# Six up-projection blocks moved into the attention, and the reordering around them

## The chip, the cores and the metric

The kernel runs on one NeuronCore of one Trainium2 chip. The metric is the device time of one execution in microseconds (us). Three runs of the kernel before gave 1068.75, 1070.24 and 1074.82 us; the median, 1070.24 us, is the time to compare with.

## The reference

Input: 4 sequences of 1024 tokens, 128 features, float32. Four residual sublayers follow one another, each `x = x + layernorm(f(layernorm(x)))`:

1. a single-head attention over channels;
2. a feed-forward layer with ternary weights and an exact gelu;
3. an attention with 16 heads of 8 features and rotary positions;
4. a mixture of 24 experts, cut to what matters here:

```python
def per_group(xf, lw, lb):                       # 4 groups of 1024 tokens
    combine, dispatch = top2_dispatch(xf, Wg, C) # softmax gates, top 2, capacity C = 86 per expert
    h = moe_apply(xf, combine, dispatch, W1, b1) # per expert 128 -> 512, summed over a token's 2 experts
    h = layer_norm(h, lw, lb)
    h = jax.nn.relu(h)
    return moe_apply(h, combine, dispatch, W2, b2)  # 512 -> 128
```

A token's hidden row is the sum of two experts' outputs, and the normalisation comes after that sum. A group is the same quarter of all four sequences.

## The kernel before, in words

The change lies in the last two stages, `second_scores` (L1581, the 16-head attention) and `expert_layers` (L1940, the experts). Each is a block with one hand-written instruction list per engine; an engine goes on to the next block when all have finished. Nothing is scheduled by a tool: the order is what the code says, and engines wait on semaphores.

**The attention** works in 8 halves (`HB`), half k being one sequence's 512 query tokens. A half has 32 steps (`G`), 8 for each of 4 units of 4 heads. I number steps through: step 32k + g. In each step TensorE computes four 128x512 score tiles (`score`, L1846, two per call), ScalarE exponentiates them in two 128x1024 instructions (L1676), and TensorE multiplies the exponentials of two steps back with the values (`av`, L1859, 8 matmul records). PSUM has 8 banks: three score buffers of two banks (`RING`), and two banks `acc` in which units accumulate in turn. VectorE copies a finished unit out of its `acc` bank, TensorE transposes it into a ring slot (L1866), VectorE divides (L1770, L1773). Four products per half, in `LATE` steps 6, 8, 22 and 25 (`late_products`, L1492 to L1496: two groups of transposes, the output projection, the gate logits), belong to the half before; the VectorE class `LateChain` continues them with two normalisations and the top-2 search (`choices`). TensorE, VectorE and SyncE issue these in order, so an instruction that waits holds all behind it.

**Routing.** `Choice` turns the expert choices of two groups into lists of rows: `prefixes`, `positions`, `gates`, `values`, `spread` on VectorE, and `position_products`, `map_products` (L1468), `last_products` (L1479) on TensorE. Its last step sets `rows_done`. Groups 0 and 1 are routed in halves 4 to 7 (`routes`, L1870), in the unused bank of an output slot; groups 2 and 3 in the expert stage, once half 7's late products and their VectorE chain are through. After routing, GpSimd gathers the input rows of the first four blocks (L1726), and SyncE loads the remaining W2 experts at the end of the attention (L1666).

**The experts** work in 24 blocks (`NU`), 6 per group (`NB`), each 4 experts of 96 rows in three 128-row tiles. For block n: GpSimd gathers its input rows (`gather_x`); TensorE transposes them (L2153) and computes the up layer (`up`, L2156: per tile 8 float32 matmul records and 4 bfloat16 bias products); ScalarE scales them by the gate into a ring of 27 row tiles in SBUF (`hidden`, L2259); SyncE stores each tile to `h_rows` in HBM. When the whole group is stored, GpSimd gathers for each row the other expert's row of that token (`partners`, L2076): in `ACCUMULATED` blocks, 0 to 5 among them, an indirect DMA adds it in place; otherwise it goes to a buffer and VectorE adds. ScalarE squares and sums (`std`, L2278), VectorE scales (`normed`), TensorE transposes (`h_transposes`), ScalarE applies scale, bias and relu (`relu`, L2291), TensorE computes the down layer (`down`, L2192, L2196), VectorE scales (`result`) and SyncE stores.

GpSimd's order is a fixed list (from L2105): x-gathers 4 to 9, partners 0 to 3, x 10, partners 4, x 11, partners 5, x 12 to 15, partners 6 and 7, and so on. TensorE's order (from L2209) interleaves up(0) to up(5) with the four late products of half 7, then up(6), positions of groups 2 and 3, up(7), up(8), routes(2), down(0), up(9), routes(3), down(1), up(10), down(2), up(11), down(3) to down(5). From down(6) on, groups overlap: three ups ahead, then one beside each of three downs.

## Time and profile before

| | us |
|---|---|
| Median of 3 runs | 1070.24 |
| Profiled execution, span on the chip | 1135.4 |
| Sublayers 1 and 2 and the projections of 3 | 0 to 239.5 |
| Attention: first exponential to the end of the last unit | 239.5 to 731.7 |
| Experts | 731.7 to 1135.4 |
| TensorE busy | 908.8 (80%) |
| ScalarE busy | 774.8 (68%) |
| VectorE busy | 580.1 (51%) |
| POOL (GpSimd) busy | 353.7 (31%) |

The profiled execution's own time is its span; it is 65.2 us longer than the median of the unprofiled runs. How to read the profile: each instruction has a start and a duration; the idle time before it is put down to the instruction or transfer whose semaphore came last; "issue" means that nothing in the profile was waited for, and "remote" that what ended the wait isn't told. PE is TensorE's matmuls and PEld its weight loads, ACT is ScalarE, DVE VectorE, POOL GpSimd. PEclk 1.00 is the full granted TensorE clock. TensorE's ends are modelled, so the distance between starts is the safer measure.

### The profile page before, as it was taken

Reading aid. Unit: us, or ns where it says so; the run is one execution under the profiler, and the core shown is the slowest. Engines: PE = TensorE matmul, PEld = TensorE weight load, DVE = VectorE, ACT = ScalarE, POOL = GpSimd, SP = SyncE. Lnnn points to the kernel's source line nnn. Section 1 sums busy time; section 2 is a strip of 40 time slices with the busy share of each in tenths; the row PEclk is TensorE's granted clock in tenths of the full one; section 3 lists DMA queues with packets and bytes.
Section 4 is the critical chain, followed back from the end, with each engine's and each line's share of the span. In section 5 each row is a group of like instructions: output and inputs, shape, how many; then the busy total and the mean of one; then the engine's idle time right before and its main releaser. Section 6 shows DMA issues by size and latency. Waiting matters only on the chain. (4 is left out here: it accounts for less than half of the span.)

```text
span 1135.4 us, 19356 instructions
## 1 busy us (share of the span) xinstructions
PE 908.8 (80%) x6642; PEld 428.2 (38%) x6642; DVE 580.1 (51%) x1969; ACT 774.8 (68%) x1130; POOL 353.7 (31%) x335
## 2 busy tenths in 40 slices
PE   3959878859999999998999999887876488477830
PEld 3745664312222222222222233224563265357730
DVE  7499998931144444444342624255214036476667
ACT  1236555789999999999999999746444254455510
POOL 6322445831000000000000013147746735365733
PEclk9669988969999999999999999998889688898975
DMA  5000001544541211212121213668747436375741
GB/s 166 1 1 1 1 1 50 130 111 153 154 118 43 61 42 40 56 36 54 44 62 44 58 36 83 184 188 198 143 127 229 88 114 178 95 192 156 144 118 51
DMA packets 91325, 106.56 MB, mean 94 GB/s; under 512 B 12957, under 2 KB 63902, under 8 KB 91114
## 3 DMA queue, kind: packets, MB, share of 16 engines
q1 hardware_dynamic: 77512, 76.83, 22.9%
q0 software_dynamic: 12224, 27.80, 12.0%
q10 hardware_dynamic: 1506, 0.89, 0.3%
q8 instruction: 44, 0.72, 0.3%
q14 instruction: 39, 0.32, 0.1%
HBM read 68.90 MB, written 36.57 MB: 93 GB/s over the span
## 5 line engine op out<-in xcount | busy, mean ns | idle before, releaser
L1676 ACT ACTIVATE s_e<-s_ps 128x1024 f32<-128x1024 f32 x512 | 476.7, 1065 | 12.3 <-PE s_ps L1846 11.5
L1859 PE MATMUL s_acc<-s_e,s_v 128*32 128x512 f32 x2048 | 274.0, 607 | 0.7 <-ACT s_e L1676 0.7
L1293 POOL DMA_INDIRECT x_in<-x_tokens,rows_of x72 | 72.2, 1003 | 458.7 <-DVE rows_of L1449 416.3
L1846 PE MATMUL s_ps<-qk 51*128 51x512 bf16 x1024 | 180.2, 387 | 23.1 <-ACT s_e L1676 10.4
L1846 PEld LDWEIGHTS s_ps<-qk 51*128 51x128 bf16 x1024 | 41.2, 93 | 272.8 <-ACT s_e L1676 252.2
L2291 ACT ACTIVATE qk<-e_pn,ln_hid 128x384 f32<-128x384 f32 x96 | 63.4, 667 | 89.7 <-remote 38.9
L2196 PE MATMUL e_py<-w,qk 128*96 128x128 f32 x768 | 112.3, 298 | 0.5 <-issue 0.5
L2166 PE MATMUL e_ph<-w,qk 128*32 128x512 f32 x576 | 84.9, 654 | 31.9 <-ACT e_hs L2259 23.9
L2196 PEld LDWEIGHTS e_py<-w,qk 128*96 128x96 f32 x768 | 101.6, 184 | 0.8 <-issue 0.8
L1293 POOL DMA_INDIRECT e_ya<-y_rows,take x64 | 63.0, 985 | 40.5 <-issue 19.4
L2259 ACT ACTIVATE e_hs<-e_ph,gate_of 128x512 f32<-128x512 f32 x54 | 36.3, 687 | 56.8 <-PE e_ph L2169 31.3
L1859 PEld LDWEIGHTS s_acc<-s_e,s_v 128*32 128x32 f32 x2048 | 40.4, 108 | 80.3 <-issue 53.5
L2180 PE MATMUL e_pn<-ident,e_hs 128*128 128x128 f32 x216 | 41.3, 313 | 35.8 <-ACT qk L2291 19.9
L1770 DVE RECIPROCAL s_rec<-s_ps 128x16 f32<-128x16 f32 x32 | 8.2, 258 | 107.6 <-PE s_ps L1866 107.5
L1293 POOL DMA_INDIRECT v_all<-h_rows,rows_of x39 | 39.1, 1002 | 75.5 <-DVE x_res L2340 21.3
L1293 POOL DMA_INDIRECT e_hs<-h_rows,rows_of x30 | 50.5, 1684 | 19.7 <-DMA h_rows<-e_hs 8.0
L1758 DVE COPY s_as<-s_acc 128x512 f32<-128x512 f32 x32 | 22.1, 689 | 65.1 <-PE s_acc L1859 64.4
L2180 PEld LDWEIGHTS e_pn<-ident,e_hs 128*128 128x128 f32 x216 | 29.3, 160 | 39.8 <-ACT qk L2291 22.0
L2269 ACT ACTIVATE l_o<-e_hs 128x512 f32<-128x512 f32 x54 | 33.7, 625 | 10.2 <-DMA e_hs<-h_rows,rows_of 5.8
L2166 PEld LDWEIGHTS e_ph<-w,qk 128*32 128x32 f32 x576 | 15.7, 114 | 64.4 <-ACT e_hs L2259 35.4
L1513 DVE COPY s_ot<-s_ps 128x512 f32<-128x512 f32 x14 | 9.7, 692 | 45.8 <-PE s_ps L1492 45.8
L2169 PE MATMUL e_ph<-bias_split,expert_hot 128*32 128x512 bf16 x288 | 31.8, 406 | 0.6 <-issue 0.6
(459 smaller groups left out, 1422.7 us busy)
## 6 DMA issues: line engine op xcount, KB each, us to landing
h_rows<-e_hs SPq DMA_DIRECT2D x54, 256.0 KB
w<-in_w SPq DMA_DIRECT2D x10, 768.0 KB, 6.1
qk<-parts_k SPq DMA_DIRECT2D x64, 96.0 KB
qk<-parts_k SPq DMA_DIRECT2D x64, 64.0 KB
h_rows<-x_res SPq DMA_DIRECT2D x16, 256.0 KB
parts_q<-b_parts SPq DMA_DIRECT2D x16, 192.0 KB, 2.8
parts_k<-b_parts SPq DMA_DIRECT2D x16, 192.0 KB, 2.8
qk<-parts_q SPq DMA_DIRECT2D x64, 48.0 KB
```

The costliest lines, as they stand in the source:

```text
L1293: nc.gpsimd.indirect_dma_start(dst, None, rows, bass.IndirectOffsetOnAxis(ap=idx, axis=0), compute_op=op).then_inc(R["landed"][k % FLIGHT] ...
L1676: nc.scalar.activation(E[g % 4][:, 2 * pair:2 * pair + 2, :], pS[BUFFER["score", 2 * g + pair]][:].rearrange("p (a s) -> p a s", a=2), ACT ...
L1758: nc.vector.tensor_copy(AS[hu % 2][:], acc[hu % 2][:]).then_inc(acc_read, 1)
L1846: last = nc.tensor.matmul(pS[BUFFER["score", 2 * g + pair]][:, a * CH:(a + 1) * CH], K[c % 2][rows, pair, j * P:(j + 1) * P], Q[c % 2][row ...
L1859: last = nc.tensor.matmul(acc[hu % 2][32 * h:32 * h + 32, :], V4[c % 2][:, j, h, :], E[g % 4][:, h, :], start=j == 0, stop=j == TB - 1)
L2166: mm(pH[m % 2][32 * q:32 * q + 32, :], XT[n % 2][:, j * P + 32 * q:j * P + 32 * q + 32], W1[:, e, :], start=True, stop=False)
L2169: last = mm(pH[m % 2][32 * q:32 * q + 32, :], I3[:, e:e + 1].broadcast_to([P, 32]), BS[:, 0:FF], start=False, stop=True)
L2180: tr = nc.tensor.transpose(pN[k % 2][:, j * P:(j + 1) * P], row(m * TPB + j)[:, c * P:(c + 1) * P], ident[:])
L2196: last = mm(out[0:ROWS, e * D:(e + 1) * D], HT[c][:, e * ROWS:(e + 1) * ROWS], W2[:, eb * EB + e, c, :], start=False, stop=c == FC - 1, sk ...
L2259: nc.scalar.activation(row(m), pH[m % 2][:], ACT.Copy, scale=G128[:, n // NB, m % NT:m % NT + 1]).then_inc(hs_done, 1)
L2269: nc.scalar.activation(squares, row(t), ACT.Square, accum_out=ssq[:, t % NT:t % NT + 1]).then_inc(sq_done, 1)
L2291: nc.scalar.activation(HT[c][:].rearrange("p (g j s) -> p j g s", g=EB, j=TPB), src, ACT.Relu, bias=lnh[:, 1, h, c:c + 1], scale=lnh[:, 0, ...
```

## The change

- The attention is unrolled from half 4 on (before: 5). In the unrolled halves the product with the values that would stand in step 8c + 2 comes one step later, so that a unit can begin in the bank that the unit before has just left; from half 4's third unit all units use `acc[0]`, and `acc[1]` is a spare bank.
- Routing of groups 0 and 1 goes through the spare bank at steps 160 to 184, in half 5; the mean-centring of W1 is spread over halves 1 to 3 (before: 1 to 4).
- From step 191 on, in three of eight steps, TensorE issues one of 24 pieces in the spare bank: for each of blocks 0 to 5 the input transposes and three up tiles. VectorE reads each piece (`up_read`): a copy, or the gate scaling into one of four staging tiles. GpSimd stores the tile to `h_rows`, and gathers x 4 to 9 there too. W2's rest is loaded at step 192.
- In the expert stage SyncE first loads the 18 tiles of blocks 0 to 5 back (`own_load`). TensorE does the late products, waits until they are read, then down(0), positions, up(6), routes(2), up(7), down(1), up(8), routes(3), up(9), down(2), up(10), down(3), up(11), down(4), down(5). The positions of groups 2 and 3 share one bank, one after the other. From block 6's down on, the order is the old one. ScalarE starts with std(0), std(1), relu(0), and VectorE interleaves `normed` and `result` with the routing.

```diff
+UB = 6
+UNROLLED = 4
+SINGLE = UNROLLED * HU + 2
+ROUTE_STEPS = {"places": (160, 162), "rows": ((170, 172), (181, 183)), "tiles": (173, 184)}
+UP_STEPS = [s for s in range(191, G * HB) if s % TB in (2, 5, 7)][:UB * (TPB + 1)]
+NST = 4
...
+        single = lambda k, hu: isinstance(k, int) and k * HU + hu >= SINGLE
+        acc_of = lambda k, hu: acc[0] if single(k, hu) else acc[hu % 2]
+        spare = acc[1]
+        XT = R["V"][:, 0:NQ].rearrange("p n t e -> p (n t e)")[:, 0:TPB * P]
+        staged = [R["X"][:, b * TB:b * TB + TH, :].rearrange("p t d -> p (t d)") for b in range(NST)]
...
+                if n == 6 * NQ + 1:
+                    sp.wait_ge(split_done, 6)
+                    sp.wait_ge(R["rows_done"], 2)
+                    w2(slice(EARLY, NE))
...
-                landed(pool, R, place("x", 0, TPB * n + TPB - 1))
+            for n in range(UB):
+                for t in range(n * TPB, (n + 1) * TPB):
+                    pool.wait_ge(u_read, t + n + 2)
+                    nc.gpsimd.dma_start(DR["h"][t // NT][t % NT, :, :], staged[t % NST]).then_inc(R["st_out"][t % NST], 16)
+                if n + NXS < 2 * NB:
+                    if n + NXS == NB:
+                        pool.wait_ge(R["rows_done"], 2)
+                    pool.wait_ge(u_mm, n * (TPB + 1) + 1)
+                    gather_x(nc, R, n + NXS)
...
+            def up_read(step):
+                if step not in UP_STEPS:
+                    return
+                i = UP_STEPS.index(step)
+                n, j = i // (TPB + 1), i % (TPB + 1) - 1
+                v.wait_ge(u_mm, i + 1)
+                if j < 0:
+                    nc.vector.tensor_copy(XT, spare[:, 0:TPB * P]).then_inc(u_read, 1)
+                    return
+                t = n * TPB + j
+                if t == 0:
+                    v.wait_ge(R["x_saved"], 16 * B)
+                if t % NT == 0:
+                    v.wait_ge(R["rows_done"], t // NT + 1)
+                if t >= NST:
+                    v.wait_ge(R["st_out"][t % NST], 16 * (t // NST))
+                nc.vector.tensor_scalar(staged[t % NST], spare[:], R["G128"][:, t // NT, t % NT:t % NT + 1], None,
+                                        ALU.mult).then_inc(u_read, 1)
...
+            def first_unit(k, at):
+                unit_read(k, 0)
+                up_read(at + 10)
+                chain.output_statistics(k - 1)
+                chain.inverse_deviation()
+                unit_output(k, 0)
+                up_read(at + 12)
+                if k == 5:
+                    choice.map_rows(0, spare)
+                chain.output_normed()
+                if k == 5:
+                    choice.last_rows(0, spare)
+                up_read(at + 13)
+                chain.residual(k - 1)
+                up_read(at + 15)
+                chain.inverse_deviation()
+                chain.normed(k - 1)
+                up_read(at + 16)
...
+                if k == 4:
+                    choice.prefixes()
+                    choice.positions(0, spare)
...
+            def fourth_unit(k, at):
+                unit_read(k, 3)
+                up_read(at + 10)
+                if k == 4:
+                    choice.positions(1, spare)
+                    choice.gates()
+                unit_output(k, 3)
+                up_read(at + 12)
+                if k == 4:
+                    choice.values()
+                up_read(at + 13)
+                if k < HB - 1:
+                    chain.read(k, 0)
+                if k == 4:
+                    choice.spread(0)
+                up_read(at + 15)
+                if k < HB - 1:
+                    chain.read(k, 1)
+                up_read(at + 16)
...
+            def route(step):
+                if step in ROUTE_STEPS["places"]:
+                    h = ROUTE_STEPS["places"].index(step)
                     pe.wait_ge(R["pf_done"], 1)
+                    if h == 0:
+                        pe.wait_ge(acc_read, SINGLE)
+                    else:
+                        pe.wait_ge(R["pos_read"], h)
...
+                        position_products(nc, R, W, spare, h, i)
+                for h in range(2):
+                    if step == ROUTE_STEPS["rows"][h][0]:
+                        pe.wait_ge(R["hot_done"], 2 * (h + 1))
+                        if h == 0:
+                            pe.wait_ge(R["pos_read"], 2)
+                        else:
+                            pe.wait_ge(R["rows_done"], h)
+                        map_products(nc, R, W, spare, h, range(GT))
+                    if step == ROUTE_STEPS["rows"][h][1]:
+                        map_products(nc, R, W, spare, h, range(GT, 2 * GT))
+                    if step == ROUTE_STEPS["tiles"][h]:
+                        last_products(nc, pe, R, W, spare, h)
...
+            def early_up(step):
+                if step not in UP_STEPS:
+                    return
+                i = UP_STEPS.index(step)
+                n, j = i // (TPB + 1), i % (TPB + 1) - 1
+                if i == 0:
                     pe.wait_ge(R["rows_done"], 2)
+                    pe.wait_ge(w1_done, NE // 3)
+                    pe.wait_ge(split_done, 6)
+                    pe.wait_ge(one_done, 4)
+                else:
+                    pe.wait_ge(u_read, i)
+                if j < 0:
+                    for t in range(TPB):
+                        landed(pe, R, place("x", n // NB, n % NB * TPB + t))
+                    for t in range(TPB):
+                        tr = nc.tensor.transpose(spare[:, t * P:(t + 1) * P], R["XS"][n % NXS][:, t, :], R["ident"][:])
+                    tr.then_inc(u_mm, 1)
+                    return
+                up_products(nc, R, spare, XT, n, j).then_inc(u_mm, 1)
...
+                    if unrolled and g % TB == 3:
+                        av(k, first, g - 3)
+                    if not unrolled and (g >= 2 or not first) or unrolled and g % TB != 2:
...
+                    if unrolled:
+                        route(k * G + g)
+                        early_up(k * G + g)
...
-            return range(m + NB, m + NR) if m % NB == 0 and m + NB < NU else ()
+            return range(m + NB, m + NR) if m in (NB, 2 * NB) else ()
 
         def beside(m):
 
+            if m < NB:
+                return {0: (6, 7), 1: (8, 9), 2: (10,), 3: (11,)}.get(m, ())
...
+            for i in range(NST):
+                sp.wait_ge(R["st_out"][i], staged_count(i, UB * TPB))
             for n in range(NB):
-                h_store(n)
-                if n == 3:
-                    token_rows(sp, R, HB - 1)
+                own_load(n)
+            token_rows(sp, R, HB - 1)
+            sp.wait_ge(R["x_out"], 16 * HB)
+            sp.wait_ge(R["x_saved"], 16 * HB)
...
+                for i in range(NST):
+                    if h < 2:
+                        pool.wait_ge(R["st_out"][i], staged_count(i, min(UB, (h + 1) * NB) * TPB))
+                if (h + 1) * NB > UB:
+                    pool.wait_ge(h_out[h], 16 * TPB * ((h + 1) * NB - max(UB, h * NB)))
                 for t in range(first * TPB, end * TPB):
                     n = kept_adds(t)
                     if t // TPB in ACCUMULATED:
                         dst, op = row(t), ALU.add
+                        if t // TPB < UB:
+                            pool.wait_ge(own_in[t // TPB], 16 * TPB)
...
-            inputs(4, 10)
...
+            def positions():
+                pe.wait_ge(R["pf_done"], 2)
+                for h in (2, 3):
+                    if h == 3:
+                        pe.wait_ge(R["pos_read"], h)
+                    for i in range(GT):
+                        position_products(nc, R, W, pM, h, i)
...
-            late(0)
-            x_transposes(0)
-            for n in range(NB):
-                up(n)
-                if n in (0, 3, 4):
-                    late({0: 1, 3: 2, 4: 3}[n])
+            for i in range(NX):
+                late(i)
+            pe.wait_ge(R["late_read"], HB * NX)
+            for c in range(FC):
+                h_transposes(0, c)
+            pe.wait_ge(R["w2_in"], 48)
             for m in range(NU):
-                for n in ahead_of(m)[0:1]:
+                for n in ahead_of(m):
                     up(n)
-                if m == 0:
-                    pe.wait_ge(R["pf_done"], 2)
-                    for h in (2, 3):
-                        for i in range(GT):
-                            position_products(nc, R, W, pY[h - 2], h, i)
-                for n in ahead_of(m)[1:]:
-                    up(n)
-                if m == 0:
-                    routes(2)
-                if m % NB == 0:
+                if m and m % NB == 0:
                     for c in range(FC):
                         h_transposes(m, c)
-                if m == 0:
-                    pe.wait_ge(R["w2_in"], 48)
                 for c in range(FC):
                     down(m, c)
-                    if m % NB < NB - 1:
+                    if m == 0 and c == FC - 1:
+                        positions()
+                        h_transposes(1, FC - 2)
+                    if m % NB < NB - 1 and (m or c != FC - 2):
                         h_transposes(m + 1, c)
-                for n in beside(m):
+                if m == 0:
+                    x_transposes(NB)
+                for i, n in enumerate(beside(m)):
                     up(n)
-                if m == 0:
-                    routes(3)
+                    if m < 2 and i == 0:
+                        routes(m + 2)
...
-            xt(0)
-            for n in range(NB):
-                hidden(n)
+            act.wait_ge(R["late_mm"], HB * NX - 3)
+            std(0)
+            std(1)
+            relu(0, NU)
             exponents(nc, act, R, 1)
-            act.wait_ge(R["late_mm"], HB * NX - 1)
-            act.wait_ge(R["x_out"], 16 * HB)
-            for h in range(GR):
+            std(2)
+            for j in range(NB):
+                if j < NB - 1:
+                    relu(j + 1, j + 3)
+                if j == 0:
+                    xt(NB)
+                for n in beside(j):
+                    hidden(n)
...
+            normed(0)
             chain.read(p, 3)
+            normed(1)
             chain.choices(p)
             choice.prefixes()
-            choice.positions(2, pY[0])
-            choice.positions(3, pY[1])
+            choice.positions(2, pM)
+            choice.positions(3, pM)
             choice.gates()
+            normed(2)
+            result(0)
             choice.values()
             choice.spread(2)
+            normed(3)
             choice.map_rows(2, pM)
             choice.last_rows(2, pM)
-            normed(0)
             choice.spread(3)
-            normed(1)
-            normed(2)
-            result(0)
+            result(1)
+            normed(4)
             choice.map_rows(3, pM)
             choice.last_rows(3, pM)
-            normed(3)
-            result(1)
-            normed(4)
+            result(2)
             normed(5)
-            for j in range(2, NB - 1):
-                result(j)
+            result(3)
```

## Rows read from the trace of the kernel before

**Rows 1.** Windows cut at the starts of halves 1, 4, 5, 6, 7: us, busy (records), PEclk, DMA, GB/s

```profile
299.50:359.40 59.90, 57.51 (x426) 14.66 (x424) 26.42 (x94) 59.41 (x65) 0.00 (x0) 1.00 0.37 103
479.40:542.60 63.20, 58.04 (x432) 14.84 (x434) 29.08 (x105) 60.27 (x67) 0.00 (x0) 1.00 0.18 47
542.60:603.00 60.40, 58.23 (x470) 15.87 (x468) 21.74 (x98) 59.49 (x65) 0.00 (x0) 1.00 0.18 50
603.00:665.40 62.40, 60.41 (x458) 17.43 (x456) 28.95 (x114) 59.64 (x65) 0.00 (x0) 1.00 0.17 48
665.40:728.30 62.90, 60.55 (x505) 17.82 (x504) 20.30 (x95) 59.88 (x65) 12.06 (x12) 1.00 0.48 125
```

**Rows 2.** Timeline, attention half 6, ScalarE and TensorE: start us, us, engine, line, operation

```profile
601.22 18.63 ACT L1676 ACTIVATE s_e<-s_ps 128x1024 f32<-128x1024 f32 x20
...
615.57 1.06 PE L1859 MATMUL s_acc<-s_e,s_v 128*32 128x512 f32 x8
...
617.10 1.06 PE L1859 MATMUL s_acc<-s_e,s_v 128*32 128x512 f32 x8
...
618.42 0.97 PEld L1494 LDWEIGHTS s_ps<-l_wo,s_ot 128*128 128x128 f32 x8 [0.23 <-issue]
```

**Rows 3.** Timeline, half 4, VectorE

```profile
535.05 1.90 DVE L1375 TENSOR_TENSOR w<-w 128x96 bf16<-128x96 bf16 x8
```

**Rows 4.** Timeline, half 6, TensorE

```profile
656.33 2.86 PE L1468 MATMUL s_ps<-w 128*96 128x72 f32 x32
```

**Rows 5.** Timeline, end of the attention, TensorE's weight loads

```profile
731.73 0.42 PEld L1492 LDWEIGHTS e_pn<-ident,l_o 128*128 128x128 f32 x4 [1.16 <-issue]
```

**Rows 6.** Timeline of the expert stage, TensorE

```profile
818.58 0.49 PE L2153 MATMUL e_px<-ident,x_in 128*128 128x128 f32 x3
819.00 1.06 PE L2166 MATMUL e_ph<-w,qk 128*32 128x512 f32 x8
...
820.10 1.04 PE L2166 MATMUL e_ph<-w,qk 128*32 128x512 f32 x8
...
822.37 0.42 PE L2192 MATMUL e_py<-bias_split,expert_hot 128*96 128x128 bf16 x4
...
827.46 0.49 PE L2153 MATMUL e_px<-ident,x_in 128*128 128x128 f32 x3
...
836.84 1.93 PE L2166 MATMUL e_ph<-w,qk 128*32 128x512 f32 x8 [6.25 <-ACT e_hs L2259]
...
851.73 3.69 PE L2196 MATMUL e_py<-w,qk 128*96 128x128 f32 x32
```

**Rows 7.** Waits of ScalarE after 731 us: us in total, times, longest us

```profile
ACT qk L2291 <- remote: 38.9, 10, 8.2
...
ACT e_hs L2259 <- remote: 24.3, 7, 7.8
```

**Rows 8.** Timeline, POOL (the waits before each in brackets)

```profile
693.86 1.42 POOL L1293 DMA_INDIRECT x_in<-x_tokens,rows_of  x1 [2.55 <-DMA x_in<-x_tokens,rows_of]
...
770.29 1.60 POOL L1293 DMA_INDIRECT e_hs<-h_rows,rows_of  x1 [7.96 <-DMA h_rows<-e_hs]
...
799.40 0.95 POOL L1293 DMA_INDIRECT x_in<-x_tokens,rows_of  x1 [0.30 <-issue]
...
842.26 0.95 POOL L1293 DMA_INDIRECT v_all<-h_rows,rows_of  x1 [7.73 <-DMA h_rows<-e_hs]
```

**Rows 9.** Timeline of the expert stage, ScalarE and TensorE's weight loads

```profile
789.38 0.30 ACT L2275 ACTIVATE gate_exponents<-gate_exponents,consts 128x3 f32<-128x3 f32 x1
...
791.95 1.72 PEld L2196 LDWEIGHTS e_py<-w,qk 128*96 128x96 f32 x8
```

**Rows 10.** Timeline of the expert stage, VectorE

```profile
763.64 0.44 DVE L1560 MAX8 l_top<-l_lg 128x8 f32<-128x24 f32 x4
...
771.76 1.02 DVE L1384 TENSOR_TENSOR v_all<-e_py,e_ya 128x384 f32<-128x384 f32 x2 [3.15 <-PE e_py L1459]
...
779.22 1.35 DVE L1430 TENSOR_TENSOR v_all<-e_ya 128x1152 f32<-128x1152 bf16 x1
```

211 lines of the change are left out of this document (99 added, 112 removed).

## The prediction

> **What bounds the kernel now.** I read the busy table in windows first, cut where the halves of the attention begin. A plain half takes 59.9 us, ScalarE busy 59.4 of it, at the full TensorE clock [rows 1]. Then the timeline of one half: 20 exponentials in 18.63 us with the last one's own 1.0, so one per about 0.92 us and 1.84 us per step [rows 2]. So ScalarE bounds the attention. TensorE is close behind: two products with the values start 1.53 us apart where nothing holds it [rows 2]. Three unrolled halves are longer than 59.9: half 4 with 63.2, half 6 with 62.4, half 7 with 62 [rows 1]. In half 4 VectorE makes the prefixes of the routing, 1.90 us for their additions alone, ahead of a unit's output [rows 3]; in halves 6 and 7 TensorE has a 2.86 us row of map products [rows 4] between scores.
>
> In the expert stage, from 731.7 us on [rows 5], nothing is busy throughout. Partners of group 0 can be gathered only when all its up tiles are stored, at 770.3; those of group 1 start at 842.3 [rows 8]. TensorE begins down(0) at 792 [rows 9] and ends down(5) at 851.73 + 3.69 = 855.4 [rows 6]. ScalarE's waits there have an odd part: 38.9 and 24.3 us on which the profile names no cause [rows 7]. The same table for the attention has none of these, and their sum, 63 us, is nearly the 65.2 us by which the profiled span exceeds the median. I take these stalls for a cost of being profiled. That matters here: a trade in the expert stage has to be made in time without them.
>
> **Step 1: what the attention pays.** A half costs TensorE 32 x 1.53 = 49.0 us, four output transposes and two transposing late products of 0.42 each (the same operation as in [rows 5]) = 2.5, and the two other late products near 1.0 each [rows 2] = 2.0: 53.5 us. An up tile costs 820.10 - 819.00 = 1.10 us, an input transpose 0.42 [rows 6].
> - Halves 6 and 7 get 18 up tiles and 5 transposes: 19.8 + 2.1 = 21.9. Together 2 x 53.5 + 21.9 = 128.9 us against 62.4 + 62.9 less 1.1 (the window of half 7 runs to the last product), 124.2 now: +4.7. TensorE is then the bound in both.
> - Half 5 gets the map products, 2 x 2.86 [rows 4], about 0.8 for the small tile products, 1.4 for the positions (my estimate, half of the late ones), one transpose: 53.5 + 8.3 = 61.8 against 60.4: +1.4.
> - Half 4 loses its stall, since the prefixes now follow the output: -3.
> - The product that waits a step puts two (2 x 1.0 us) between the two scores of step 8c + 3. The ring holds ScalarE's work for at most two exponentials, 1.84 us. Halves 4 and 5, where TensorE has room otherwise, may lose 0 to 1 us in each of 8 units; I take 0.4, +3.
>
> Sum: **+6**. Bounds: 0 if the doubled products and half the pieces fit where TensorE waits now; +15 if VectorE's read of the spare bank holds TensorE by a further 0.4 us in each of 24 pieces. VectorE reads 18 x 0.7 + 6 x 0.5 = 16 us more, in program order with a chain of some 4 us between two unit reads; it is under half busy (29 of 62 us [rows 1]), and pieces stand over 3.7 us apart, so I expect little of it. SyncE's W2 load moves from behind the last q/k loads to before them; DMA is 0.17 busy in half 6 [rows 1], and a load has a whole unit, 15 us, so I cost it at nothing. Without that room the next unit's scores would wait for it.
>
> **Step 2: the store path.** GpSimd is idle in halves 4 to 6 [rows 1]; it gets 18 stores and 18 more gathers there. A gather occupies it up to 1.42 us in the attention [rows 8]. A block, 3 stores and 3 gathers, must take less than four pieces, 10.7 steps or 21 us; at 1.42 + 0.3 each it is 10. It costs nothing. The Trainium skill speaks against it (SBUF — State Buffer, the trap "DVE blocks DMA"): a DMA issued by GpSimd that takes 620 ns alone took about 3100 ns beside VectorE copies. By that page, an estimate, a block would take 6 x 3.1 = 18.6 us and still fit, barely. No row here shows such a wait, so the rival that uses it gets little.
>
> **Step 3: the expert stage before, without the stalls.** From 731.7: one up block with its transpose takes 822.37 - 818.58 = 3.8 us, a down block with the next transposes 827.46 - 822.37 = 5.1 [rows 6]. Six ups and the late products, 22.8 + 3.3, and about 5 for the last scaling and store put the partners' start at 763 (trace: 770.3). From that start to the square root of block 1 took 789.4 - 770.3 = 19.1 us, and 2.6 more to down(0) [rows 8, 9]: 784.7. down(0) 5.1; then up(9) waits for gather x 10, which stands behind 12 partner gathers: the trace has its last issue 29.1 us after the first partner [rows 8], so 792, landed at 796.5; up(9) 3.8, routes(3) 3.4, four more downs 20.4 and two ups 7.6, less what already overlaps, plus some 4 for x 11: down(5) ends at about 836, the partners of group 1 start at about 825. The trace has 855.4 and 842.3: 19 and 17 us of stalls in the first 124 of 404 us, in proportion to 63.
>
> **Step 4: the same with the change.** The stage begins at 731.7 + 6 = 737.7. What is late next is the round trip: group 0's tiles are in HBM and must come back. Three 256 KB loads with their latency, about 5 us (estimate), then the same 19.1 + 2.6: down(0) at 764.4, 20 us earlier. But only six ups are done, where before nine were. The routing now sets the pace: VectorE needs normed(1) (1.5), then from choices to spread(2) what the trace takes, 779.22 + 1.35 - 763.64 = 16.9, less its 3.15 wait [rows 10], plus about 3 for positions one after the other in one bank and 2.2 for normed(2) and result(0): 782.5. TensorE has down(0), positions and up(6) in that time, 11 us of 18, and waits. Then routes(2) 3.5, five ups 19.0, five downs 25.5, routes(3) 3.4: 834; down(5) ends there, and the partners of group 1 start after up(11), at about 827.
> The idle 20 us at the start also cools TensorE: after 6.25 us of idle an up tile took 1.93 instead of 1.06 us [rows 6], and the granted clock is at its lower level, 1.2 GHz, for the first few microseconds. +2 us. So 836 against 836, 829 against 825.
>
> Nothing behind it changes in kind: block 6 needs TensorE free, which weighs as much as the partners. I take the end of down(5): **0 us**. Against the median: **1070**. A measurement of this kernel tells about 0.5% (5.3 us) from no change.
>
> **The rivals.**
> - *The stalls are the kernel's own* (or shrink with the stores that leave). Then before is 855.4 as traced, and after has its 97 us of path from 737.7, plus 10 rather than 19 of stalls: 845, so -10, 1060. For it: the stalls stand beside heavy DMA traffic, and 4.6 MB of stores leave the stage. Against: equally many bytes are loaded back, and the sum of 63 fits the profiling. Some gain would also come from the attention's lower bound (0, not +6). Together **0.36**, from 1052 to 1064.9.
> - *TensorE-bound attention with held reads*, the one on the other side. Place: halves 6 and 7, where TensorE no longer has room. If a piece waits for VectorE's read, 24 x 0.4 = 9 more; the attention is then 15 longer, 1079; to 1086 if the round trip also meets its own loads, 18 of them in a row, and takes 7 more. It decides from 0.25 us per piece. For it: VectorE's order is fixed, and `up_read` waits for a piece while the chain behind it waits. Against: pieces are spaced. **0.25.**
> - *The GpSimd path fills* (the page's rule): a block over 21 us would stop staging, reads, and TensorE; at 4 us each six operations take 24, 3 us per block, 15 in all: 1085. **0.02.**
> - *It doesn't do what it says*: the ups could stand in the attention and still end later than it. Program order excludes that: the expert block starts only when TensorE has issued all 24 pieces, so it would show as a longer attention, and is in the second rival.
>
> My forecast, an even trade within 0.5%, has **0.37**. Its own range is 1065 to 1076. The whole range holds the first rival's 1056 and most of the second's: **1056 to 1083**. Outside it lie about 0.08 below and 0.08 above. Faster by over 0.5%: 0.36; within: 0.37; slower: 0.27 (0.25 + 0.02).
>
> **What the profile of the changed kernel would show.**
> - Half 4 near 60 us, halves 6 and 7 near 65 each, with ScalarE waiting for scores and TensorE's starts without gaps. Halves of 60 would mean step 1 is too dear; waits of TensorE for `up_read` would make the second rival.
> - No TensorE work between the late products and down(0) but transposes, about 20 us, and a PEclk under 1.0 there. First partner gather about 5 us after the stage begins, down(0) 26 to 27 us after it.
> - TensorE waiting for spread(2) ahead of routes(2), rows_done for group 2 about 50 us into the stage.
> - down(5) ending about 97 us after the stage's start, plus stalls. If this is under 90, step 4 is wrong; if the whole stage after it is shorter or longer than before's 280 us (1135.4 - 855.4), I have missed what follows.

## The result, and the profile after

The changed kernel takes 1086.84 us, the median of four runs (1081.79 to 1090.62), against 1072.2 of four of the kernel before: 1.0147 of it, 95% interval 1.0114 to 1.0179. I had forecast 1070.0 with 1056 to 1083. In a later comparison on the same kind of chip it was 1.0156 (1.0126 to 1.0187). The profiled execution took 1081.79 us with a span of 1079.9, so its parts add up without the 65 us that stood between trace and median before. It is the fastest of the four, though, 5 us under their median.

First the windows of the plain half 1 and of halves 4 to 7 of after, cut at the same exponentials as [rows 1]:

```profile
core 0: us, PE busy (x) PEld busy (x) DVE busy (x) ACT busy (x) POOL busy (x), PEclk, DMA share, GB/s
296.50:356.40 59.90, 57.58 (x426) 14.70 (x424) 26.42 (x94) 59.41 (x65) 0.00 (x0) 1.00 0.34 103
476.40:537.10 60.70, 57.19 (x446) 15.43 (x445) 22.42 (x101) 60.16 (x66) 0.00 (x0) 1.00 0.18 50
537.10:602.80 65.70, 63.78 (x572) 22.57 (x568) 32.95 (x129) 60.52 (x66) 12.50 (x12) 1.00 0.23 57
602.80:672.50 69.70, 68.58 (x545) 18.56 (x541) 27.81 (x102) 61.58 (x66) 12.91 (x17) 1.00 0.51 151
672.50:742.20 69.70, 68.50 (x544) 18.07 (x536) 27.05 (x100) 61.58 (x65) 13.85 (x18) 1.00 0.27 76
```

Half 4 fell from 63.2 to 60.7 us, half 5 grew from 60.5 to 65.7, halves 6 and 7 from 62.4 and 62.8 to 69.7 each. In these two TensorE is busy for all but 1.1 us, at the full clock, while ScalarE, which bounds half 1, is idle for 8 us. VectorE is busy for 28 of 69.7 us. What TensorE waits for in half 6, and how long (summed us, times, longest), is one row, and none of it is a wait for VectorE's reads:

```profile
PE s_ps L1955 <- ACT s_e L1701: 1.0, 3, 0.5
```

The timeline of TensorE's matmuls in half 6 shows what one piece costs (start, duration, line, operation, count):

```profile
603.01 0.60 PE L1955 MATMUL s_ps<-qk 51*128 51x512 bf16 x4
603.55 1.06 PE L1968 MATMUL s_acc<-s_e,s_v 128*32 128x512 f32 x8
...
611.32 0.66 PE L1975 MATMUL s_ps<-ident,s_as 128*128 128x128 f32 x4
611.91 0.39 PE L1955 MATMUL s_ps<-qk 51*128 51x512 bf16 x2
612.23 1.06 PE L1968 MATMUL s_acc<-s_e,s_v 128*32 128x512 f32 x8
613.22 0.39 PE L1955 MATMUL s_ps<-qk 51*128 51x512 bf16 x2
613.54 1.07 PE L1317 MATMUL s_acc<-w,v_all 128*32 128x512 f32 x8
614.43 0.40 PE L1320 MATMUL s_acc<-bias_split,expert_hot 128*32 128x512 bf16 x4
614.76 0.39 PE L1955 MATMUL s_ps<-qk 51*128 51x512 bf16 x2
615.08 1.06 PE L1968 MATMUL s_acc<-s_e,s_v 128*32 128x512 f32 x8
```

Read distances between starts. Four scores side by side take 603.55 - 603.01 = 0.54 us. An up tile (L1317 and L1320) takes 614.76 - 613.54 = 1.22, and it stands between two pairs of scores: they take 2 x 0.32 (613.22 to 613.54, 614.76 to 615.08) instead of 0.54. Together 1.32 us. The output transposes take 0.59 and split the scores in the same way.

Then the expert stage, TensorE's matmuls at its start and at down(5):

```profile
744.20 0.66 PE L1975 MATMUL s_ps<-ident,s_as 128*128 128x128 f32 x4 [0.81 <-DVE s_as L1786]
747.48 0.82 PE L1512 MATMUL e_pn<-ident,l_o 128*128 128x128 f32 x4 [2.63 <-PEq L1603]
749.09 2.08 PE L1514 MATMUL e_pn<-l_wo,v_all 128*128 128x128 f32 x8 [0.78 <-DVE v_all L1533]
763.53 1.12 PE L1512 MATMUL e_pn<-ident,l_so 128*128 128x128 f32 x4 [12.36 <-DVE l_so L1572]
...
794.01 4.05 PE L1488 MATMUL e_pm<-v_all 128*96 128x72 f32 x32 [3.05 <-DVE v_all L1450]
...
843.74 3.69 PE L2328 MATMUL e_py<-w,qk 128*96 128x128 f32 x32
```

and GpSimd's first partner gather:

```profile
754.40 1.62 POOL L1301 DMA_INDIRECT e_hs<-h_rows,rows_of  x1 [6.14 <-DMA e_hs<-h_rows]
```

The stage's start (L1512, the row that answers to [rows 5]) is at 747.48, the first partner 6.9 us behind it, the end of down(5) at 847.43, 99.95 us behind. For 12.36 us TensorE waits for VectorE's chain. In the 28.1 us from the stage's start to down(0) it is busy for 8.8, so idle for 19.3, at a granted clock of 0.51; I had forecast about 20 us idle and a clock under 1.0.

These lengths need a trace of before without the stalls of [rows 7]. It came with the experiments: prefixes_2 below is the kernel before with one VectorE step moved, and differs from it in half 4 alone (60.6 instead of 63.2). Its rows of TensorE:

```profile
726.28 0.63 PE L1492 MATMUL e_pn<-ident,l_o 128*128 128x128 f32 x4 [0.94 <-PEq L1583]
...
828.72 3.69 PE L2196 MATMUL e_py<-w,qk 128*96 128x128 f32 x32
```

| us | before | after | difference | forecast |
|---|---|---|---|---|
| halves 4 and 5 | 123.7 | 126.4 | +2.8 | +1.4 |
| halves 6 and 7 | 125.2 | 139.5 | +14.3 | +4.7 |
| end of the last exponential to the stage's start | 3.5 | 5.2 | +1.7 | 0 |
| stage's start to end of down(5) | 106.1 | 99.95 | -6.2 | -6 |
| from there to the end | 230.6 | 232.5 | +1.9 | 0 |

(The first three lines of before are from its own trace, the last two from prefixes_2: 832.41 - 726.28, 1063.0 - 832.41.) The sum is +14.5 us, and 1.47% of 1070 is 15.7. The last line is the least certain. The trace of after_2 below, a run at its kernel's median, has the same attention and the same 99.9 us to down(5), but 236.5 us from there to the end instead of 232.5, and the other kernels with six blocks in the attention have 235.8 to 237.8 on that kind of chip (piece_beside, ups_first, both_edits). Kernels with the old stage have 230.6 (prefixes_2) and 232.9 (reorder_spread). So behind down(5) the changed kernel more likely loses some 4 us than 2. Why, no run here tells. The switch of blocks is longer because TensorE idles 2.63 us for its own queue there (the row at 747.48) and 0.94 in the other kernel.

### The profile page after: what moved, and what is told of

Read it like the earlier page. It is cut to its first block and busy times, and to the rows that moved or that the text cites. A ratio compares the mean times of both kernels' runs of the same rounds, so it can differ in the third digit from the quotient of the medians.

```text
span 1079.9 us, 19334 instructions
## 1 busy us (share of the span) xinstructions
PE 888.2 (82%) x6642; PEld 418.2 (39%) x6642; DVE 598.5 (55%) x1993; ACT 766.9 (71%) x1108; POOL 365.5 (34%) x353
## 5 line engine op out<-in xcount | busy, mean ns | idle before, releaser
L1968 PE MATMUL s_acc<-s_e,s_v 128*32 128x512 f32 x2048 | 270.6, 606 | 0.5 <-ACT s_e L1701 0.4
L2328 PE MATMUL e_py<-w,qk 128*96 128x128 f32 x768 | 104.0, 284 | 0.0
L2328 PEld LDWEIGHTS e_py<-w,qk 128*96 128x96 f32 x768 | 93.8, 172 | 0.0
L1301 POOL DMA_INDIRECT e_ya<-y_rows,take x64 | 65.6, 1025 | 32.5 <-issue 25.3
L1317 PE MATMUL e_ph<-w,qk 128*32 128x512 f32 x432 | 62.6, 654 | 7.3 <-ACT e_hs L2396 5.5
L1756 POOL DMA_DIRECT2D h_rows<-x_res x18 | 10.2, 564 | 127.6 <-DVE x_res L1816 127.6
L2396 ACT ACTIVATE e_hs<-e_ph,gate_of 128x512 f32<-128x512 f32 x36 | 24.4, 688 | 16.9 <-PE e_ph L1320 15.9
L2483 DVE TENSOR_TENSOR e_hs<-e_hs,v_all 128x512 f32<-128x512 f32 x24 | 16.2, 691 | 26.9 <-DMA v_all<-h_rows,rows_of 26.8
L759 PEld LDWEIGHTS a_po<-down_t,f_h 128*128 128x128 f32 x256 | 29.7, 192 | 2.9 <-issue 2.9
```

What stands on the lines that cost most here:

```text
L759: last = mm(pD[k % 2][:, j * P:(j + 1) * P], H[:, k % 2, f, j * P:(j + 1) * P], R["down_t"][:, f * P:(f + 1) * P], start=f == 0, stop=f == ...
L1301: nc.gpsimd.indirect_dma_start(dst, None, rows, bass.IndirectOffsetOnAxis(ap=idx, axis=0), compute_op=op).then_inc(R["landed"][k % FLIGHT] ...
L1317: nc.tensor.matmul(bank[32 * q:32 * q + 32, :], XT[:, j * P + 32 * q:j * P + 32 * q + 32], R["W1"][:, e, :], start=True, stop=False)
L1968: last = nc.tensor.matmul(acc_of(k, hu)[32 * h:32 * h + 32, :], V4[c % 2][:, j, h, :], E[g % 4][:, h, :], start=j == 0, stop=j == TB - 1)
L2328: last = mm(out[0:ROWS, e * D:(e + 1) * D], HT[c][:, e * ROWS:(e + 1) * ROWS], W2[:, eb * EB + e, c, :], start=False, stop=c == FC - 1, sk ...
L2396: nc.scalar.activation(row(m), pH[m % 2][:], ACT.Copy, scale=G128[:, n // NB, m % NT:m % NT + 1]).then_inc(hs_done, 1)
```

## The experiments

The theory (A): the loss is made in the attention by TensorE's own time, since halves 6 and 7 became TensorE-bound and each piece costs more than its duration; the expert stage gives what I forecast up to down(5). Rivals: the reordering itself costs (C), the pieces wait for VectorE's read (D), the stalls of ScalarE (E). Further letters are explained in the expectation in which they stand.

**Two kinds of chip.** The comparisons ran on chips of two kinds. On one the kernel before took 1128.33 us (median of 23 runs, 1121 to 1140), on the other 1070.08 (19 runs, 1065 to 1075). I tell the kinds apart by this time alone; all comparisons of the slower kind are of one chip. The ratios below are to the kernel before on the same chip.

**The kernel before again.** No edit.

> The kernel before, unchanged, for a trace that can be compared with that of after. Theory A (the 15 us are lost in the attention, which grew from 487.7 to 504.7 us between first and last exponential; the expert stage is an even trade): the attention takes 487 to 489 us again, without a stall without a named cause in the expert stage, and the expert stage, from the last unit's transposes to the end, takes about 332 us, as it does after. Rival B (the expert stage lost too, or gained and gave part back): that stage takes under 328 or over 337 us here.

Measured: 1127.57 us. The waits of ScalarE in its trace, the answer to [rows 7] (summed us, times, longest):

```profile
ACT qk L2291 <- remote: 42.4, 12, 10.3
...
ACT e_hs L2259 <- remote: 25.5, 9, 6.4
```

The stalls are back, and on this chip all other runs take about 1128 us too. None of the eight traces of the faster kind, which are profiled as well, has a row with "remote". So the stalls are a matter of the chip or its state, not of profiling; the trace of before that I had read shows the same stalls and length. The attention took 488.6 us between first and last exponential, as expected; the stage can't be compared on this chip.

**The reordering alone, without pieces.** The attention of after without a piece, the expert stage of before, and GpSimd waits after each of its first gathered blocks, as in before.

```diff
-UP_STEPS = [s for s in range(191, G * HB) if s % TB in (2, 5, 7)][:UB * (TPB + 1)]
+UP_STEPS = []
...
             for n in range(NXS):
                 gather_x(nc, R, n)
+                landed(pool, R, place("x", 0, TPB * n + TPB - 1))
```

> The reordered attention of after (unrolled from half 4, one accumulator bank and a spare one, the two products of the values in steps 8c + 3, routing of groups 0 and 1 through the spare bank in half 5, prefixes behind the output), with no up tile in it; the expert stage is that of before. Theory A (the inserted pieces make the loss): half 4 stays near 60.7, half 5 near 65, halves 6 and 7 fall from 69.7 to 60 us each; the whole 3 us under before, ratio 0.997. Rival C (the doubled products and the single accumulator make it): halves 6 and 7 stay above 63 us, the whole at 1075 or more.

Measured (slower chip): 0.9949 (0.9912 to 0.9986). Halves 6 and 7:

```profile
606.80:667.00 60.20, 56.69 (x426) 14.94 (x424) 19.74 (x90) 59.69 (x66) 0.00 (x0) 1.00 0.47 128
667.00:727.00 60.00, 56.05 (x422) 14.73 (x420) 19.54 (x89) 59.49 (x65) 0.00 (x0) 1.00 0.14 39
```

The doubled products, the single accumulator and the W2 load at step 192 cost nothing there; C is out. Half 5 took 68.8 us, 3 more than in after; on the faster chip it was never over 65.7 in any kernel.

**The map products spread over two halves.** The same, with the steps of group 1's map products moved by 32 and the W2 load at the end again.

```diff
-ROUTE_STEPS = {"places": (160, 162), "rows": ((170, 172), (181, 183)), "tiles": (173, 184)}
+ROUTE_STEPS = {"places": (160, 162), "rows": ((170, 172), (213, 215)), "tiles": (173, 216)}
```

> The reordered attention without the pieces, as before, with the map products of group 1 in half 6 instead of half 5, and the load of the rest of W2 at the end of the attention again. Theory A: half 5 falls from 65 (68.8 as run) to about 62.5, half 6 grows from 60.1 to about 62.5, since what counts is the ring running dry at each row of 1.4 us; the whole equals reordering alone or is 1 to 3 us shorter, 0.993 to 0.997 of before. Rival C (half 5 is long because TensorE has too much to do there in all): the two halves together lose 4 us or more.

Measured (faster chip): 0.9979 (0.9959 to 0.9999), halves 5 to 7 of 62.4, 63.4 and 60.3 us. The two halves lose 2.4 + 3.4 = 5.8 us over 60, as much as half 5 of after alone. That passes the 4 us which I had put down as the sign of rival C (too much TensorE work in half 5), but my own theory gave some 5, so the sign couldn't tell them apart. What speaks against C is that half the work in each of two halves costs as much as all of it in one. My 62.5 for half 6 was low, and nothing is gained: behind each map row of 1.43 us ScalarE waits 0.9 to 1.2 us, about 1.1, wherever it stands. That is what is left of 1.43 if the ring refills by only 1.84 - 1.53 = 0.3 us per step (an estimate). In before an undivided row of 2.86 us costs 2.4 a half. Splitting rows saved nothing, and the 5.7 us of half 5 are for the most part the price that halves 6 and 7 had paid before.

**Up tiles without their float32 products.**

```diff
-    for q, e in enumerate(experts):
+    for q, e in enumerate(experts if full else ()):
         nc.tensor.matmul(bank[32 * q:32 * q + 32, :], XT[:, j * P + 32 * q:...], R["W1"][:, e, :],
```

> After, but the 18 up tiles in the attention consist of their bfloat16 bias products alone: the eight float32 matmul records of each tile, the product of the tokens with W1, are left out, so the hidden rows of blocks 0 to 5 hold the bias only. Everything that waits, reads, stores and gathers stays. Theory A (TensorE's own time is the price, with what a change of shape costs it): a tile gets cheaper by about 0.85 us and there are 9 in each of halves 6 and 7; these fall from 69.7 to about 62, at most 7.7 less each, and the whole is 15 us under after, near 1071. Rival D (the wait for VectorE's read of the spare bank, or its place in VectorE's order, is the price): the halves stay above 66 us and the whole above 1080.

Measured (slower chip): 0.9979 (0.9937 to 1.0021). Windows of halves 5 to 7, and one tile in TensorE's timeline:

```profile
539.00:618.80 79.80, 66.93 (x571) 22.85 (x567) 33.02 (x129) 61.10 (x66) 11.55 (x12) 0.89 0.20 47
618.80:681.20 62.40, 60.72 (x473) 17.14 (x469) 27.71 (x102) 60.51 (x65) 12.92 (x17) 1.00 0.57 168
681.20:743.80 62.60, 60.76 (x472) 16.74 (x464) 26.94 (x100) 60.65 (x65) 13.86 (x18) 1.00 0.30 85
```

```profile
628.92 0.40 PE L1320 MATMUL s_acc<-bias_split,expert_hot 128*32 128x512 bf16 x4
629.26 0.39 PE L1955 MATMUL s_ps<-qk 51*128 51x512 bf16 x2
```

A tile is 0.34 us instead of 1.22: 9 x 0.88 = 7.9 us less work per half, and the halves fell by 7.1 to 7.3. What TensorE is spared comes off by nine tenths, with every wait, read, store and gather still there. Half 5 (79.8 us here, clock 0.89) is taken up under two_blocks.

**Each tile read twice by VectorE.**

```diff
+                nc.vector.tensor_copy(junk[:], spare[:])
                 nc.vector.tensor_scalar(staged[t % NST], spare[:], R["G128"]...).then_inc(u_read, 1)
```

> After, but VectorE reads each of the 18 up tiles in the spare bank twice, the first time into scratch space, and says only then that the bank is free: some 0.65 us more per tile, 12 us more of VectorE. Theory A: TensorE is the bound and a piece stands over 3.7 us behind the one before, so nothing or up to 2 us is added. Rival D (the pieces wait for VectorE's read): the 0.65 us come back for most of 18 tiles, 8 to 12 us.

Measured (slower chip): 1.0147 (1.0093 to 1.0202). Halves 6 and 7 in windows:

```profile
618.70:688.50 69.80, 68.68 (x545) 18.64 (x541) 33.10 (x111) 61.68 (x66) 12.56 (x17) 1.00 0.51 150
688.50:758.20 69.70, 68.51 (x544) 18.16 (x536) 32.35 (x109) 61.57 (x65) 13.85 (x19) 1.00 0.26 77
```

VectorE does 5.3 us more per half than in after and the halves stay at 69.7. TensorE's waits in half 6 are those of after, 1.0 us in three pieces for ScalarE, and none for the reads. D, the mechanism of my second rival, is out.

**After again**, beside the next ones on the faster chip.

> After, unchanged, beside the kernels of this comparison, on a chip where the kernel before may take longer for the stalls of ScalarE. All theories: halves 6 and 7 at 69.7 us. Theory A: the loss of the attention is there whatever the chip, so the ratio is 1.005 to 1.02. Theory E (the first profile of before was of a chip with these stalls, and what a kernel loses to them depends on where its GpSimd gathers stand): halves 4 and 5 or the expert stage differ from the first trace of after by 5 us and more where ScalarE waits without a named cause.

Measured: 1.0156 (1.0126 to 1.0187), 1087.6 us; all halves as in the first trace within 0.1 us, down(5) ends 99.9 us behind the stage's start. No ScalarE wait without a cause, so E's difference isn't seen between two chips of this kind.

**Pieces next to the products with the values.**

```diff
                         av(k, first, g - 2)
+                    if unrolled:
+                        early_up(k * G + g)
                     score(k, first, g, 1)
...
                         route(k * G + g)
-                        early_up(k * G + g)
```

> After, but each of the 24 pieces is issued right behind the product with the values (in steps 8c + 2, which have none, between the two scores) instead of behind the step's second score, so that the scores of two steps stay next to each other and a float32 128 x 32 product follows one of the same shape. Theory A (a piece costs TensorE 0.2 us more than its own time, for the change of shape and for the scores that no longer overlap): 12 pieces in each of halves 6 and 7 get 0.15 to 0.25 us cheaper, these halves fall from 69.7 to 66.7 to 67.9, the whole by 4 to 6 us. Rival F (the halves are long by the pieces' own time and by waits for ScalarE's tiles): no change, within 0.5 us per half, or slower since the second score comes later in the step.

Measured: 1.0077 (1.0050 to 1.0105), 1080.4 us. Halves 6 and 7 took 67.2 us. The timeline of half 6:

```profile
620.20 1.06 PE L1968 MATMUL s_acc<-s_e,s_v 128*32 128x512 f32 x8
...
621.08 1.04 PE L1317 MATMUL s_acc<-w,v_all 128*32 128x512 f32 x8
...
622.27 0.61 PE L1955 MATMUL s_ps<-qk 51*128 51x512 bf16 x4
622.81 1.07 PE L1968 MATMUL s_acc<-s_e,s_v 128*32 128x512 f32 x8
```

The product with the values is 0.88 us to the next start instead of 0.99 (612.23 to 613.22 above), the tile 1.19, and the scores stay four in 0.54. So a tile costs 1.19 - 0.11 = 1.08 instead of 1.32 us, 9 x 0.24 = 2.2 of the 2.5 us per half. The rest of the 7 us of the whole was unexpected: down(5) ended 96.2 us behind the stage's start instead of 99.9, with no edit there. The map row of routes(2), here and in after_2:

```profile
791.45 2.94 PE L1488 MATMUL e_pm<-v_all 128*96 128x72 f32 x32 [1.00 <-DVE v_all L1450]
795.73 3.94 PE L1488 MATMUL e_pm<-v_all 128*96 128x72 f32 x32 [3.36 <-DVE v_all L1450]
```

It took 2.94 us at a granted clock of 1.00 where it follows 1.00 us of idle; in after_2 it follows 3.36 us and took 3.94, at 0.70, and the 6 us behind it stood at 0.65. From this row to down(1), the same instructions, piece_beside takes 7.7 us and after_2 10.6: these 2.9 us of clock are most of the 3.7, and behind down(1) the two run alike.

**up(6) and up(7) into the wait at the stage's start.**

```diff
-            for i in range(NX):
-                late(i)
+            late(0)
+            late(1)
+            x_transposes(NB)
+            up(NB)
+            up(NB + 1)
+            late(2)
+            late(3)
```

> After, with up(6) and up(7) moved from behind the positions and routes(2) to the start of the expert stage, into the 12.4 us that TensorE waits there for the chain of VectorE; they fit, since the first seven halves of x are saved at the end of the attention. The attention does not change. Theory A (after down(0) TensorE's list of products is the path to down(5): five ups, five downs, two routings behind spread(2)): down(5) ends 4 to 8 us earlier than in after (100 us behind the stage's start), and so does the kernel. Rival G (routing on VectorE and the partner gathers on GpSimd set the pace up to down(5)): under 2 us.

Measured: 1.0091 (1.0060 to 1.0121), 1081.5 us. TensorE's wait of 12.36 us has gone:

```profile
763.80 0.40 PE L1320 MATMUL e_ph<-bias_split,expert_hot 128*32 128x512 bf16 x4
764.37 0.66 PE L1512 MATMUL e_pn<-ident,l_so 128*128 128x128 f32 x4 [0.17 <-DVE l_so L1572]
...
796.10 1.24 PE L1488 MATMUL e_pm<-v_all 128*96 128x72 f32 x6 [5.57 <-DVE v_all L1450]
```

The stage began at 748.76, down(5) ended at 840.24 + 3.69 = 843.93, 95.2 us behind it instead of 99.9: 4.7 us, of 7.6 moved. The third row shows where the rest went: routes(2) now waits 5.57 us for spread(2), with nothing left to do meanwhile. Both the products behind down(0) and the routing of VectorE set the pace, and my G (the routing sets it) is right for what goes beyond 4.7.

**Both edits, first on the slower chip.** The two diffs above together.

> After with both edits: pieces right behind the products with the values, and up(6), up(7) at the start of the expert stage. Theory A (the two act in different stages): halves 6 and 7 at 67.2 us as with the first alone, down(5) ends 95 us or less behind the stage's start as with the second alone; 10 to 13 us under after, 1.003 to 1.007 of before. Rival H (both repair the same thing, the cold clock of TensorE behind the wait of 12 us): 7 to 8 us under after.

Measured: 1.0105 (1.0058 to 1.0152), halves 6 and 7 of 67.2 and 67.5 us. Down(5) ended 108.5 us behind the stage's start there, with stalls of ScalarE inside, in a run 12 us above the median, so this says little on the stage.

> The kernel of beside_and_first again. On a chip without the stalls, theory A: 10 to 13 us under after, 1.002 to 1.006 of before; rival H (both edits repair the cold clock): 1.007 to 1.009. On a chip with them only the halves 6 and 7 and the first 100 us of the stage can be read.

Measured (faster chip): 1.0053 (1.0032 to 1.0073), 1076.7 us. Halves 67.2 each, down(5) 94.9 us behind the start. Against 1.0156 that is 1.03% or 11 us. The halves keep their 5.0. In the stage the two together give 5.0, where the one alone gave 4.7 and the other 3.7: there both repair partly the same thing, as H says, and A holds for the attention. The row of routes(2) shows how: it took 5.39 us behind 5.71 of idle, at a clock of 0.50, as in ups_first, so that nothing is left of piece_beside's warm row. The 11 us of the whole fit A's 10 to 13.

**The prefixes behind the output of unit (4, 2), in the kernel before.**

```diff
-                    if (k, hu) == (4, 2):
-                        choice.prefixes()
                     v.wait_ge(tr_mm, k * HU + (hu + 1))
...
                                         ALU.mult).then_inc(o_done, 1)
+                    if (k, hu) == (4, 2):
+                        choice.prefixes()
```

> The kernel before with one edit: the prefixes of the routing behind the output of unit (4, 2) instead of ahead of it. All theories: half 4 from 63.2 to 60 to 60.7 us, nothing else moves; the whole 2.5 to 3 us under before, 0.997, that is, all of what the reordered attention brings.

> The kernel of prefixes again. Half 4 at 60.6 us and the others as in before, the whole at 0.997 of before on a chip without stalls; theory E: the stalls of ScalarE stay away or come as they do for before.

Measured: 0.9944 (0.9900 to 0.9989) on the slower chip, 0.9972 (0.9954 to 0.9990) on the faster, where it took 1067.36 us. Half 4 fell to 60.6 us, the others stayed: 2.6 us for one moved call, as much as the whole reordered attention brings without pieces.

**Two blocks instead of six.** Eight pieces, in step 8c + 2 of halves 6 and 7, between the two scores. The expert stage computes the other four blocks first, takes up(6) to up(8) ahead of down(0), and puts normed(0) and normed(1) ahead of spread(2).

```diff
-UB = 6
-UP_STEPS = [s for s in range(191, G * HB) if s % TB in (2, 5, 7)][:UB * (TPB + 1)]
+UB = 2
+UP_STEPS = [s for s in range(191, G * HB) if s % TB == 2][:UB * (TPB + 1)]
...
+            late(0)
+            x_transposes(UB)
+            for n in range(UB, NB):
+                up(n)
+                if n == UB:
+                    late(1)
+            late(2)
+            up(NB)
+            late(3)
+            up(NB + 1)
+            positions()
+            up(NB + 2)
...
+                if m == 0:
+                    routes(2)
+                for n in beside(m):
+                    up(n)
+                if m == 0:
+                    routes(3)
```

> Two blocks instead of six in the attention: eight pieces, one per unit, each in step 8c + 2 between the two scores, where no product with the values stands. up(2) to up(5) in the expert stage with the late products between them, up(6) to up(8) behind, then down(0), routes(2), up(9), routes(3), and on as before. Theory A (up to 4 pieces per half fit into the 4 us that TensorE has over; what costs is the pieces above that): halves 6 and 7 at 60 to 61.5 us, the first partner gather 22 to 25 us behind the stage's start instead of 35, down(5) 96 to 100 us behind it instead of 106, the whole at 0.990 to 0.996 of before. Rival G (the routing chain of VectorE sets the pace and the gain is given back behind down(5)): 0.996 to 1.000.

Measured (slower chip): 0.9989 (0.9942 to 1.0036), no change clear of noise. Halves 6 and 7 took 61.3 us, as expected, but half 5 took 79.8. So did it in every kernel on this chip that issues the first 12 gathers in a row (bias_tiles, twice_read, beside_and_first), against 68.8 in reorder_only, which waits for each block, and 65.7 in all of them on the faster chip. In twice_read ScalarE's rows there are:

```profile
576.88 1.94 ACT L1702 ACTIVATE s_e<-s_ps 128x1024 f32<-128x1024 f32 x2 [4.55 <-remote]
585.48 3.77 ACT L1702 ACTIVATE s_e<-s_ps 128x1024 f32<-128x1024 f32 x4 [6.66 <-remote]
```

Both waits begin within the row of gathers (568.2 to 583.1). So I let GpSimd wait for each block again:

```diff
             for n in range(NXS):
                 gather_x(nc, R, n)
+                landed(pool, R, place("x", 0, TPB * n + TPB - 1))
```

> Two blocks in the attention as in two_blocks, and the first 12 gathers of GpSimd in half 5 wait for each block to land again, as in the kernel before (after lets all 12 go in a row). Theory A: halves 6 and 7 at 61.3 us, down(5) 96 to 101 us behind the stage's start on a chip without stalls of ScalarE (106 in the reordered kernel without pieces), the whole at 0.990 to 0.997 of before. Theory E (on a chip with the stalls, the row of 12 gathers brings 14 us of them into half 5): half 5 near 66 to 69 us on either chip, against 79.8 for the row of 12 on the chip with stalls. Rival G (given back behind down(5)): 0.997 to 1.001.

Measured (faster chip): **0.9915** (0.9892 to 0.9939), 1061.57 us, faster than both kernels. The windows of halves 5 to 7:

```profile
538.90:604.60 65.70, 63.78 (x572) 22.40 (x567) 32.40 (x128) 60.53 (x65) 14.17 (x12) 1.00 0.23 57
604.60:665.90 61.30, 60.41 (x465) 15.97 (x463) 22.49 (x94) 59.78 (x65) 4.65 (x6) 1.00 0.52 142
665.90:727.30 61.40, 59.93 (x461) 15.74 (x459) 22.29 (x93) 59.88 (x65) 4.64 (x6) 1.00 0.19 54
```

and TensorE at the stage's start and at down(5):

```profile
730.93 0.63 PE L1512 MATMUL e_pn<-ident,l_o 128*128 128x128 f32 x4 [0.94 <-PEq L1603]
...
772.06 3.18 PE L2322 MATMUL e_pn<-ident,e_hs 128*128 128x128 f32 x12 [6.25 <-DVE e_hs L2506]
...
821.37 3.69 PE L2338 MATMUL e_py<-w,qk 128*96 128x128 f32 x32
```

The middle row is TensorE's longest wait on the way, 6.25 us for the scaling of block 0 ahead of down(0). Four pieces a half cost 1.2 us over the 60.1 without any; twelve in the same place, between the two scores, cost 7.1 (67.2 in piece_beside), and 9.6 where after has them. The partners start 23.5 us behind the stage's start (32.6 in prefixes_2, 6.9 in after), down(5) ends at 94.1 instead of 106.1. The whole, against the same two traces as in the table: attention and switch +0.7 (492.9 against 492.2 from the first exponential to the stage's start), -12.0 up to down(5), +3.3 behind it (233.9 against 230.6): -8.0, and 0.85% is 9.1. Of these, some 3 us are the moved prefixes, which this kernel has too: against prefixes_2, which took 1067.36 us on the same chip, it wins 5.8 us. Whether pacing removes the 14 us on the slower chip wasn't tried: this run was on the faster one.

## Why the prediction was wrong

Step 1 failed: its term for halves 6 and 7, 64.5 us each, measured 69.7, which is 10.4 of the 16.8 us that were missing (1086.8 - 1070). The price of a piece in its place had been taken too low. Half 5 adds 3.9 (65.7 - 61.8), the switch of blocks 1.7. Step by step:

- *Step 1, halves 6 and 7: wrong in size.* The mechanism was right (TensorE the bound, full clock, nearly no gaps), the term was 64.5 us per half and measured 69.7. I took durations from stretches in which TensorE does the same thing over and over, and none for going from one to the other. An up tile was 1.10 and is 1.32 with the scores that it parts (9 x 0.22 = 2.0); output transposes were 0.42 and are 0.59, plus 0.10 for the parted scores (4 x 0.27 = 1.1); the late products and the input transposes lose in the same way (about 1.5 together, my estimate from the same distances). With 1.1 us of waits for ScalarE that is 5.7, against 5.2 missing. piece_beside and bias_tiles show the main part of it. I also took 1.1 us from the old half 7 without need: the window ends at the last exponential (728.3), not at the last product (729.3). The old halves were 125.2, so my own sum gave +3.7 and not +4.7.
- *Step 1, half 5: wrong.* I summed TensorE's time, 61.8, but a row of 1.43 us takes 1.1 us from ScalarE even where TensorE has room later, since the ring holds two exponentials and refills by 0.3 us a step. reorder_spread shows it. TensorE's own time was short as well: it is busy for 63.8 of the 65.7 us. *Half 4* was right: 60.7.
- *The doubled products*, +3: wrong, the runs show no cost. Half 4 has them and takes 60.7 against 60.6 in prefixes_2, which has not; halves 6 and 7 of reorder_only take 60.1 us.
- *The bounds 0 to +15* left out the term that decided, the price of a piece in its place. The attention with its switch of blocks became 18.8 us longer. 15 of these I had allowed for another cause, held reads, which twice_read excludes: the second rival named the right place (halves 6 and 7), the right sign and nearly the right time, 1079 to 1086, with the wrong mechanism, so that its time was luck.
- *Step 2* was right. A GpSimd store occupied it for 0.56 us and landed in 2.4, beside VectorE's reads. The 3.1 us each that I took from the Trainium skill (SBUF — State Buffer, the trap "DVE blocks DMA") weren't seen. That is no contradiction: the page ties the wait to VectorE's copies of float32 from SBUF to SBUF, while `up_read` reads a PSUM bank, and such copies take only 2.0 us in halves 6 and 7 together (7 of 0.28 us). No run here tests the page's case.
- *Step 3* was right about the lengths (104.3 us up to down(5), 106.1 measured), wrong in its reason. The stalls weren't a cost of being profiled; they belong to one kind of chip. Scaling them by their share was luck.
- *Step 4* was right within 2 us: 98.3 us up to down(5), 99.95 measured; the first partner 6.9 us behind the start (forecast 5), down(0) 28.1 (26 to 27), the idle time ahead of it and the low clock (0.51). The wait for spread(2) ahead of routes(2) was 3.1 us where I had 7. So the expert stage gave its 6 us up to down(5), and the attention took 18.8 with the switch of blocks, to which I had given nothing (1.7).
- *The first rival* (1060) didn't come: on a chip without stalls there is nothing of them to save, and the attention was far from its lower bound. On the slower kind its saving is there: from the stage's start to the end bias_tiles and twice_read took 382.0 and 378.6 us, before_2 392.9 and reorder_only 397.6 (beside_and_first, in a run 12 us above its median, 393.9). Half 5 gave it back there with its 14 us. These are single traces with stalls of varying length, so the size is uncertain.
- *What I expected behind down(5)*, 280 us as in the old trace, is 230.6 to 232.9 without stalls. After has 232.5 and 236.5 in its two traces: "nothing behind it changes in kind" left out about 4 us of loss, and its cause stays open.

## What to carry to other kernels

Work that is moved into a stage where a second engine is nearly the bound costs little within that engine's room, and nearly its full price above it: four pieces a half cost 1.2 us, twelve in the same place 7.1, and sparing TensorE 7.9 us there gave 7.1 to 7.3. Price a piece in its place, by the distance between starts across each switch, not by its duration among its like, and put it next to work of the same form. And before a stall in a profile is explained or scaled away, look whether the other runs of that chip have it.

## What was not expected of the hardware

- Two forms of matmul in turn cost time that neither shows among its like: from the start of a product with the values (eight float32 records, 128x512 in, weights of 32 columns) to the next start it is 0.88 us where an up tile's float32 products of the same form follow, and 0.99 where bfloat16 scores follow; four scores together took 0.54 us instead of 2 x 0.32.
- The same program takes 1070 us on one kind of chip and 1128 on another, at the same attention. The difference is in ScalarE's waits without a named cause (68 us in before_2, the two rows above). A row of 12 indirect gathers brought such waits of 4.55 and 6.66 us into the attention there and none on the other. What ScalarE waits for the profile doesn't tell, and it stays open.
- A wait of TensorE of a few microseconds can cost nearly as much again: the map row of routes(2) took 2.94 us behind 1.00 us of idle (granted clock 1.00), 3.94 behind 3.36 (0.70), and in ups_first 5.39 behind 5.57, all of it at 0.50, that is at 1.2 GHz. With what stands behind the row, the 3.36 us of after_2 cost 2.9 more than the 1.00 of piece_beside. So piece_beside won in a stage that it doesn't touch.
